# Maxima of a windowed-attention kernel: two direct row writes against one store and one load through DRAM, and their matmuls two tiles earlier

## The reference

```
x = x + conv3x3(group_norm(x), W)            # 32 groups
x = x + neighbourhood_attention(group_norm(x), w_qkv, b_qkv, rpb, w_proj, b_proj)
```

## Time and profile before

| | |
|---|---|
| runs | 1427.41, 1421.59 us; median 1424.5 us |
| profiled execution | 1432.87 us, span 1431.1 us |
| busy | PE 81%, PE weight loads 57%, DVE 62%, ACT 47%, POOL 42% |
| mean granted TensorE clock | 0.859 |
| chain that ended last | PE 53%, DMA 26% (of it area<-mcol 22%), DVE 9%, issue 6%, SP's queue 4% |

### The profile page before, as it was taken

How to read it: one execution, slowest core, us unless ns; L and a number is a source line. 1 busy time by engine, 2 the same in 40 slices (tenths; PEclk the granted TensorE clock), 3 DMA queues, 4 the chain that set the end, 5 groups by cost and what they waited for, 6 DMA issues and landing times.

```text
span 1431.1 us, 38250 instructions
## 1 busy us (share of the span) xinstructions
PE 1158.9 (81%) x12441; PEld 811.7 (57%) x12441; DVE 880.3 (62%) x2129; ACT 674.5 (47%) x1867; POOL 593.9 (42%) x1278
## 2 busy tenths in 40 slices
PE   3799998556888788778979887888789788879882
PEld 3455555444666556556656664666556566656661
DVE  3422222696777576667757674767577676757671
ACT  2100000703565556565746655565557465655651
POOL 3000000500746455454636462646455454637461
PEclk7799999556899897889989997999888889989996
DMA  9200000241547374645555464657375554645472
GB/s 253 56 35 34 34 34 34 74 99 20 144 103 177 80 179 104 140 113 125 144 107 142 101 161 76 156 100 171 82 181 127 113 141 96 157 98 144 98 179 51
DMA packets 142497, 159.57 MB, mean 112 GB/s; under 512 B 29952, under 2 KB 119888, under 8 KB 142040
## 3 DMA queue, kind: packets, MB, share of 16 engines
q1 hardware_dynamic: 141432, 153.13, 45.3%
q0 software_dynamic: 864, 3.90, 0.8%
HBM read 86.09 MB, written 70.47 MB: 109 GB/s over the span
## 4 chain that ended last, share of the span: by engine, by line
PE 53%; DMA 26%; DVE 9%; issue 6%; SPq 4%; ACT 0%; POOL 0%; DVEq 0%; POOLq 0%; ACTq 0%
DMA area<-mcol 22%; PE PS L1080 13%; PE PS L1185 11%; PE PS L1148 9%; PE PS L1169 5%; PE PS L1092 4%; PE PS L1162 3%; DVE bias L933 3%; PE PS L1133 3%; PE PS L1195 3%; DVE area L975 2%; DMA area<-x 2%; SPq L423 1%; SPq L444 1%; DVE mcol L986 1%
## 5 line engine op out<-in xcount | busy, mean ns | idle before, releaser
L570 POOL TENSOR_TENSOR halves<-masked 128x96 f32<-128x96 f32 (+1 forms) x512 | 203.5, 397 | 493.3 <-DVE masked L1007 492.7
L1148 PE MATMUL PS<-area 97*128 97x48 bf16 (+1 forms) x4112 | 257.8, 211 | 138.9 <-DMA area<-mcol 119.7
L996 DVE TENSOR_TENSOR S<-PS,bias 128x384 f32<-128x384 f32 (+1 forms) x513 | 283.9, 554 | 121.2 <-PE PS L1148 115.9
L746 ACT ACTIVATE VT<-PS 128x128 f32<-128x128 f32 x449 | 126.2, 281 | 418.2 <-PE PS L1133 416.0
L1185 PE MATMUL PS<-S,VT 128*64 128x96 f32 (+1 forms) x4096 | 310.5, 278 | 0.0
L1148 PEld LDWEIGHTS PS<-area 97*128 97x128 bf16 x4112 | 186.6, 105 | 217.2 <-issue 158.9
L753 ACT ACTIVATE S<-S 128x384 f32<-128x384 f32 (+1 forms) x512 | 274.7, 539 | 46.5 <-DVE S L996 33.3
L1185 PEld LDWEIGHTS PS<-S,VT 128*64 128x64 f32 x4096 | 207.1, 148 | 143.5 <-issue 91.7
L1007 DVE TENSOR_TENSOR masked<-PS,cst 128x192 f32<-128x192 f32 (+1 forms) x512 | 181.6, 355 | 101.2 <-PE PS L1185 95.2
L986 DVE TENSOR_REDUCE mcol<-PS 128x6 bf16<-128x480 f32 (+2 forms) x297 | 181.5, 611 | 96.2 <-PE PS L1169 96.1
L1080 PE MATMUL PS<-area 128*128 128x392 f32 x576 | 192.0, 496 | 3.9 <-DVE area L875 3.9
(11 more groups left out here) (87 smaller groups left out, 1142.3 us busy)
## 6 DMA issues: line engine op xcount, KB each, us to landing
k_parts<-area SPq DMA_DIRECT2D x204, 168.0 KB, 4.1
area<-k_parts SPq DMA_DIRECT2D x33, 1008.0 KB, 8.3
q_parts<-area SPq DMA_DIRECT2D x204, 98.0 KB, 2.3
area<-q_parts SPq DMA_DIRECT2D x66, 294.0 KB, 5.9
xa<-x_mid SPq DMA_DIRECT2D x18, 392.0 KB, 6.6
late<-x_mid SPq DMA_DIRECT2D x17, 392.0 KB, 8.8
out<-area SPq DMA_DIRECT2D x17, 392.0 KB, 8.5
den<-sums SPq DMA_DIRECT2D x66, 98.0 KB
```

The costliest lines, as they stand in the source:

```text
L570: nc.gpsimd.tensor_tensor(h, m[:, :, 0:2, :], m[:, :, 2:4, :], ALU.add).then_inc(s["half"], 1)
L996: nc.vector.tensor_tensor(S[:, n % 4, 0:cols], PS[:, SCORE + n % 2, 0:cols], bias[:, at:at + cols], ALU.add).then_inc(s["biased"], 1)
L1148: last = mm(PS[:, SCORE + n % 2, cols * g:cols * (g + 1)], key_rows[a][0:PEAK_ROW + 1, g, key:key + 128], query_rows[a][0:PEAK_ROW + 1, g, ...
```

## The change

The direct write of the maxima into the row, a DMA of 128 pieces of 42 numbers and one of 128 pieces of 7 numbers, is replaced by two DMAs: `mcol` goes to a DRAM tensor `peaks` as it stands, SP waits until that has landed, and the row is then loaded from `peaks` as one run of 6272 numbers. Both issues stand where the old ones stood in SP's order. The semaphore `middle_in` goes, `peak_stored` comes. All nine banks must be done before the store, and DVE waits for the store's landing before it writes bank 0 of the next chunk. Bank b moves from tile 3 + b to tile 1 + b, and the spreads move two tiles earlier.

```diff
-        SPREAD = ({12: (0, 1), 13: (2,), 14: (3,), 15: (4,), 0: (8, 9, 10), 1: (11, 12, 13), 2: (14, 15)},
...
+        SPREAD_FROM = 10
+        SPREAD = ({10: (0, 1), 11: (2,), 12: (3,), 13: (4,), 14: (8, 9), 15: (10, 11, 12), 0: (13, 14, 15)},
...
-        FIRST_BANK, RECIPROCAL, NORMALIZE, NEXT_IMAGE, RESIDUAL = 3, 6, 12, 30, 20
+        FIRST_BANK, RECIPROCAL, NORMALIZE, NEXT_IMAGE, RESIDUAL = 1, 6, 12, 30, 20
...
-            def move_maxima(j, c, middle):
-
-
-                banks, patches = ((CHUNK_BANKS, slice(OUTER_PATCHES, PATCHES)) if middle
-                                  else (CHUNK_BANKS - 2, slice(0, OUTER_PATCHES)))
-                wait(sp, "peak_out", c * CHUNK_BANKS + banks, j)
-                row = query_rows[c % 2][PEAK_ROW:PEAK_ROW + 1].rearrange("o g h q t -> o (g h q) t")
-                sp.dma_start(row[:, :, patches], mcol[:, patches]).then_inc(s["middle_in" if middle else "rows_in"], 16)
+            def move_maxima(j, c):
+
+                wait(sp, "peak_out", (c + 1) * CHUNK_BANKS, j)
+                sp.dma_start(peaks[c % 2], mcol[:, :]).then_inc(s["peak_stored"], 16)
+                wait(sp, "peak_stored", 16 * (c + 1), j)
+                sp.dma_start(query_rows[c % 2][PEAK_ROW:PEAK_ROW + 1].rearrange("o g h q t -> o (g h q t)"),
+                             peaks[c % 2].rearrange("(o p) t -> o (p t)", o=1)).then_inc(s["rows_in"], 16)
...
-                if c and b == CHUNK_BANKS - 2:
-                    wait(dve, "middle_in", 16 * c, j)
+                if c and b == 0:
+                    wait(dve, "peak_stored", 16 * c, j)
...
-                if n == 2:
-                    wait(pe, "middle_in", 16 * (c + 1), j)
```

More of the change, by code:

```diff
@@ L219, in build @@
     k_parts = nc.dram_tensor("k_parts", (2, 2, len(PAIRS), HEAD_DIM, HEAD_PAIRS, 2 * CHUNK_KEYS), BF16, kind="Internal").ap()
+    peaks = nc.dram_tensor("peaks", (2, 128, PATCHES), BF16, kind="Internal").ap()
     sums = nc.dram_tensor("sums", (2, 8, 2 * CHUNK_Q), F32, kind="Internal").ap()
@@ L306, in build @@
                   "value_out": 1, "summed": 1, "normed": 1, "out_done": 1}
-        EACH = {"misc_in": 20, "misc_out": 20, "rows_in": 4 * ROWS_IN, "middle_in": 64, "scores": 64, "biased": 64, "probs": 64,
+        EACH = {"misc_in": 20, "misc_out": 20, "rows_in": 4 * ROWS_IN, "peak_stored": 64, "scores": 64, "biased": 64, "probs": 64,
                 "weighted": 64, "selected": 64, "half": 64, "summed": 64, "qbd": 4, "qbd_too": 4, "peak_in": 4 * CHUNK_BANKS,
@@ L341, in build @@
         MISC_PROJECT, MISC_TURN = 13, 24
-        SPREAD = ({12: (0, 1), 13: (2,), 14: (3,), 15: (4,), 0: (8, 9, 10), 1: (11, 12, 13), 2: (14, 15)},
-                  {12: (0,), 13: (1,), 14: (2,), 15: (3,), 0: (9, 10), 1: (12, 13), 2: (14, 15)})
-        SPREAD_TOO = ({12: (5,), 13: (6, 7)}, {12: (4,), 13: (5,), 14: (6, 7), 0: (8,), 1: (11,)})
+        SPREAD_FROM = 10
+        SPREAD = ({10: (0, 1), 11: (2,), 12: (3,), 13: (4,), 14: (8, 9), 15: (10, 11, 12), 0: (13, 14, 15)},
+                  {10: (0,), 11: (1,), 12: (2,), 13: (3,), 14: (9, 10), 15: (12,), 0: (13, 14, 15)})
+        SPREAD_TOO = ({10: (5,), 11: (6, 7)}, {10: (4,), 11: (5,), 12: (6, 7), 13: (8,), 14: (11,)})
         def spread_for(split, a, late):
-            return [h for n, heads in split[1 - a if late else a].items() for h in heads if (n < 12) == late]
-        FIRST_BANK, RECIPROCAL, NORMALIZE, NEXT_IMAGE, RESIDUAL = 3, 6, 12, 30, 20
+            return [h for n, heads in split[1 - a if late else a].items() for h in heads if (n < SPREAD_FROM) == late]
+        FIRST_BANK, RECIPROCAL, NORMALIZE, NEXT_IMAGE, RESIDUAL = 1, 6, 12, 30, 20
         K_PIECE, Q_PIECE = CHUNK_KEYS // 2, CHUNK_Q
@@ L502, in _ @@
             load_residual(IMAGES - 1)
-            move_maxima(None, 0, False)
-            move_maxima(None, 0, True)
+            move_maxima(None, 0)
             sp.wait_ge(s["scores"], 1)
@@ L517, in _ @@
                         fill_queries(j, c + 1)
-                    move_maxima(j, c + 1, False)
-                    move_maxima(j, c + 1, True)
+                    move_maxima(j, c + 1)
                     if c % 2 == 0:
@@ L815, in _ @@
                         if n in SPREAD_TOO[c % 2]:
-                            spread_too(j, c + 2 if n >= 12 else c + 1, SPREAD_TOO[c % 2][n])
+                            spread_too(j, c + 2 if n >= SPREAD_FROM else c + 1, SPREAD_TOO[c % 2][n])
             keep_projection(None, 2 * IMAGES)
@@ L1034, in _ @@
                         if n in SPREAD[c % 2]:
-                            spread(j, c + 2 if n >= 12 else c + 1, SPREAD[c % 2][n])
+                            spread(j, c + 2 if n >= SPREAD_FROM else c + 1, SPREAD[c % 2][n])
                         if FIRST_BANK <= n < FIRST_BANK + CHUNK_BANKS:
```

## The result

The changed kernel takes 1502.36 us (1499.66 and 1505.06), against 1424.5 us before: 1.0518 times as long, 95% interval 1.045 to 1.0586. The forecast of 1517 us, slower, was met, within its range. Its sum was not met: one of its terms was 60 us too large and the others together 40 us too small, so that the nearness of the figure is largely luck. The profiled execution took 1505.06 us, span 1503.2.

A forecast was written before the change was run, and what follows sets the result against it. PE's wait for the maxima, queued behind the keys in the rings, was taken as the bound; 53 + 34 + 5 = 92 us on the 1424.5 us median gave 1517 us, range 1460 to 1570.

The forecast's parts named there:

- The bound: Loop from maxima landing through PE's restart, reciprocals and keys to the next landing; PE stands still about 3.6 us per chunk.
- The store waits behind the keys: In the DMA rings, the store queues behind the keys like the old write, landing 0.5 us earlier; forecast's chance 0.54.
- the row write itself costs: Rival: small pieces into one partition cost 3 us and small DMAs can pass the keys; 1339 us, chance 0.06.
- the store passes the keys: Rival: keys land as late as the maxima did, load and SP's issues are hidden; 1424.5 +/- 15 us, chance 0.08.
- The landing term, 33 x 1.6 = 53 us: First score matmuls start 1.6 us later in each of 33 chunks, 53 us; ends 10 and 109 us.
- the slow-load rival: Row load not shared over DMA engines, or slow into one partition: 3.3 us per chunk, 1572 us, chance 0.12.
- Only the landing counts: Rival: late stores are absorbed by room at the last stores' waits and reciprocals; 53 to 58 us, about 1480, chance 0.20.
- the estimate made from it, 69 us: Store and load through DRAM priced by the skill page: store saves nothing, 33 x 2.1 = 69 us.
- SP behind the new wait, 34 us: In 16 even chunks SP's delayed stores make the keys leave 2.1 us later, 34 us; ends 0 and 48.
- The moved maxima, 5 us: Two more maxima, fewer spreads between restart and reciprocals: 0.3 us in 16 odd chunks, 5 us; ends 0 and 19.

The follow-up runs named there:

- the early keys: Kernel before the change, with the keys of even chunks issued ahead of the reciprocals: 1423.1 us, ratio 0.9962.
- the DRAM half alone: Changed kernel with banks and spreads back in their old tiles, maxima still stored to DRAM and loaded as one run: 1474.7 us, ratio 1.0367.
- the tiles alone: Kernel before the change, with banks and spreads two tiles earlier and the direct writes kept: 1470.3 us, ratio 1.0306.
- all is moved early: Kernel before the change, with banks and spreads two tiles earlier, reciprocals in tile 5, even chunks' keys ahead of the reciprocals: 1427.2 us, ratio 0.9986.
- hold: Kernel before the change, with SP issuing nothing in all chunks until the direct maxima writes have landed: 1493.6 us, ratio 1.0461.

## Why the prediction was right, point by point

*The bound.* Right. The loop from restart to reciprocals, keys, maxima and restart is the kernel's clock; what lengthens it shows in the time. Taking PE's wait at its end away did not give its whole length, as the early keys showed.

*The store waits behind the keys.* Right, and with it the rivals fell in which the row write itself costs or the store passes the keys: it took 7.9 us from issue to landing above, and 2.5 with free rings.

*The landing term, 33 x 1.6 = 53 us.* This is the mis-sized step. The load's size was right, 2.1 us from landing to scores, but not its reason: I took 2.0 because 16 long pieces would carry it, and it went as a single packet. That was the condition of the slow-load rival, which had 3.3 us for it; the rival was right on the packet and wrong on the price. The store lands 2.1 (A) and 2.3 us (B) sooner than the old write, where I took 0.5 and gave 1.4 as the end. I had looked at the two transfers and not at what stood around them. About 1 us is that SP is silent behind the store, so that image and parts no longer share the DMA engines with the last keys and queries; 0.8 to 0.9 us is that no row writes run beside them, and 0.3 to 0.4 us that the landing follows the last packet sooner. The term is -0.1 in A and -0.3 in B. "Only the landing counts" had it the wrong way round.

The Trainium skill's fixed 2.0 us per DMA ("DMA: Bandwidth & Descriptors", the anatomy of one DMA, which it describes for DMAs that GpSimd issues) is near the load's 2.1 us. But it prices a DMA alone: the estimate made from it, 69 us, stands against a step that cost nothing.

*SP behind the new wait, 34 us.* The place was right, DVE's wait at the reciprocals included (15 waits). The size is 3.0 us in A by the DRAM half alone, 16 x 3.0 = 48 us, the upper end of my bounds. I gave 12.6 us to the twenty stores; they took 14.5 (7.20 + 7.33). In an odd chunk the slack absorbed the wait, as forecast.

*The moved maxima, 5 us.* Alone they cost 42 us (36 by profile), in B 1.3 us ahead of the keys. Here the step itself failed, and not only its size: I priced DVE's instructions, maxima against spreads, where PE sets the pace. One B cycle from its first score matmul to the reciprocals, before and with the tiles alone (stretch and its length; busy us and number of PE, PE's weight loads, DVE, ACT, POOL; granted clock, DMA share, GB/s):

```profile
673.56:690.07 16.51, 16.51 (x195) 11.34 (x196) 11.78 (x30) 12.91 (x43) 6.15 (x17) 0.90 0.23 45
...
684.74:703.46 18.72, 18.72 (x210) 12.91 (x211) 11.48 (x27) 12.53 (x42) 6.14 (x17) 0.84 0.20 40
```

In the mean of the B cycles PE is busy for 18.1 of 19.4 us before and for 19.4 of 20.8 with the tiles alone; DVE for 11.5 us in both, though it has two more maxima and, in B, five fewer spreads (the prediction had two to three). What came in are the 14 matmuls of two banks, 1.2 us of PE in the mean (the pair shown lies further apart, by its clocks of 0.90 and 0.84 too). The spreads' going gave nothing, because DVE had room: its gaps right after a restart, in the kernel before, end on PE.

```profile
644.57 0.36 DVE L1007 TENSOR_TENSOR masked<-PS,cst 128x192 f32<-128x192 f32 x1 [1.88 <-PE PS L1185]
644.85 0.31 DVE L975 TENSOR_SCALAR area<-area,cst 128x392 bf16<-128x392 bf16 x1
645.07 0.55 DVE L996 TENSOR_TENSOR S<-PS,bias 128x384 f32<-128x384 f32 x1
646.27 0.42 DVE L1007 TENSOR_TENSOR masked<-PS,cst 128x256 f32<-128x256 f32 x1 [0.65 <-PE PS L1185]
```

In A the same 14 matmuls come in, but with the tiles alone PE also had the lower clock (1.2 GHz) for 5.7 us of this stretch instead of 3.9, so that there the 1.2 us have two parts that I can't tell apart; in B these figures are 7.8 and 7.5 us. In A the delay mostly lies beside SP's: 3.3 us together, 3.0 and 1.1 alone.

Together: -7 for the landing, 48 for SP, 5 more in A and 15 x 1.5 = 23 in B for the tiles, 3 outside these 31 cycles, 72 us; the forecast had 53 + 34 + 5 = 92. Errors of 60 and 40 us partly cancelled, and the figure was better than its working. The mean granted clock fell from 0.859 to 0.828; it stood at the lower level for 10.3 us of a cycle A instead of 5.4, and for 12.4 of B instead of 10.6, a part of it in PE's waits. What that cost has no term in this sum: it lies within the distances measured.

What is open: by what the row writes hold back the keys and queries. Nor did I find what sets cycle B once all is moved early; the denominators' store by POOL and SP's waits for POOL are candidates beside PE's wait before the projection, and no run tells them apart.

## What to carry to other kernels

A wait on an in-order queue costs what stands behind it, and pays back what its silence leaves to transfers in flight; price both before you price the transfer. Work moved ahead costs if it crosses the instruction on which a loop of dependences turns, even where the engine of that instruction is far from busy; look for it (here DVE's reciprocals) and for the engine that sets the pace up to it (here PE), and move it along. And before you count a wait as a gain, ask which wait takes its place: the 2.0 us at the end of even chunks were worth 0.7.

## What the runs showed of the hardware that I had not expected

The 12.5 KB run travels whole rather than in sixteen shares: the trace has 33 packets of 12,544 bytes, one for each load, of 0.7 us. It still landed and released PE in 2.1 us, while 128 pieces of 98 bytes into the same partition took 3.5.

Row writes of 256 small pieces (84 and 14 bytes) ended 0.1 us behind the 1 MB of keys ahead of them, but the keys' own last packet came 0.9 us sooner where no row write followed (B, hold against DRAM alone).

SP's first ten stores took 6.26 us to issue while the keys' rings were full ahead of them, but 7.20 when only the image load stood ahead of them (the second ten 7.05 and 7.33). I expected the opposite and have no run on it.
